# Toeplitz loads issued by ScalarE instead of SyncE, and the wait for a last store moved into the next phase

## The chip, the cores and the metric

The kernel runs on one core of a Trainium2 chip. Its time is the device time of one execution in microseconds, the median of several runs. All five engines are used: TensorE (PE) for matrix products and transposes, VectorE (DVE), ScalarE (ACT), GpSimd (POOL), and SyncE (SP), which only issues transfers. ScalarE and GpSimd issue transfers too, each over its own queue.

## The reference, cut to what matters

`x` is 8 x 256 x 512. Four residual blocks follow one another:

```
x = x + tanh(g_xattn[0]) * conv_mix(ctx, ctx, layernorm(x), ssm_kernel, D)      # long convolution, 32 heads of 8 channels (8 x 32 = 256), over the last axis
x = x + tanh(g_ffn[0])   * moe(layernorm(x))        # 8 experts, top 2, and a shared expert
x = x + tanh(g_xattn[1]) * linear_attention(layernorm(x), ctx)
x = x + tanh(g_ffn[1])   * soft_moe(layernorm(x))

conv_mix: kv[i,j] = k[i] * v[j] per head;  y = causal convolution of kv[i,j] with the head's kernel, over the last axis
          out = sum over i of (y[i,j] + kv[i,j] * D) * q[i]
moe:      w = two largest softmax router scores, normed to 1
          out = sum over the two experts of w_e * (silu(x @ gate_e) * (x @ up_e)) @ down_e  +  shared expert(x)
```

The change touches the first block and the seam between the shared expert and the routed experts of the second. What is computed stays the same.

## The kernel before, in words

The phases run one after another, each in a block of its own: every engine has its own program in it, and the next phase begins when all five have come to the end of theirs.

**Convolution stage** (`conv_stage`, from L142). The convolution is a matrix product with a Toeplitz matrix, built by a transfer that reads the reversed kernel of a head once per partition, each time one element further on (`toeplitz`, L229). One such transfer brings the rows of one step: two heads, high and low fp16 halves, 512 KB into one of the two buffers of `toep`. There are 16 steps. Per step:

- VectorE makes the products of channel pairs (`pairs`, L400 and L402), two steps ahead.
- ScalarE rounds them to fp16 (`split`, L346, `prod_hi`), GpSimd makes the remainder (L304, `prod_lo`).
- TensorE convolves in four blocks m = 0 to 3, of 6, 12, 18 and 24 products (`convolve`, L511 to L513). Block 0 alone waits for the step's Toeplitz rows (L503) and for `prod_lo` (L504). After each block comes an `add_up` (L524) of the block two before. Results go through a ring of three PSUM buffers. In steps 1 to 4 there are also transposes of the later inputs (L496).
- VectorE weighs each block with the query (`weigh`, L428 to L431) and after the third block of a step adds the rows of the step before to the residual (`add_rows`, L440, semaphore `added`).
- Beside this, 24 pieces of the routed experts' down weights are split: GpSimd loads them (L287), ScalarE rounds (`split_parts`, L354), GpSimd makes the remainder (L293) and stores (L295).

The order in each queue is written out by hand. SyncE's is L268 to L273. In step s it issues the Toeplitz load of step s + 2, once step s has been convolved (`conv_done`); then, once `added` says so, the eight stores of step s (L255) and the eight residual loads of step s + 2 (L246). ScalarE's is L364 to L373: root or transposed inputs in a few steps, `split(s + 2)`, `split_parts(s)`. The first two Toeplitz loads it issues itself, at the start (L330).

**Shared phase** (`shared_phase`, from L553). Four chunks of 512 tokens go through the shared expert. In the last one VectorE also works out the routing: `choose`, `lay_out`, `slots` (each slot's number, and `behind`, a comparison of 128x1280 elements, L869), then, after the chunk's last `h` (L913), `places`, and `tokens` (L881), which feed the list of tokens (L1008) that the experts gather by. ScalarE rounds `h` to `h_hi` (L747), GpSimd makes `h_lo` (L782), and TensorE's last products (L1001 to L1003) need it. `add_out` (L897, L899) ends a token tile, and SyncE stores a chunk of four (L702). `x1_in` holds the chunks with odd number, the last among them. At the end SyncE waits for all these stores (L703) and those of the normed rows (L704).

**Expert phase** (`expert_phase`, from L1012). 39 tiles of 128 gathered rows (L1085) are transposed by a transfer (L1263) and go through their expert. What the shared phase stored last is read only by the phase after it.

Of the kernel before, what the change touches and what calls it, by code (L numbers as in the profile page):

```python
# [15 lines left out]
ALU = mybir.AluOpType  # L16
AX = mybir.AxisListType

P = 128
B, N, D = 8, 256, 512  # L20
T = B * N
TT = T // P
KD = D // P
CH = 4 * P
NCH = T // CH
# [93 lines left out]
STEPS = SSM_H // 2  # L119
# [22 lines left out]
def conv_stage(nc, k, x, ctx, ssm_reversed, ssm_d, g_xattn, g_ffn, ssm_split, x1, down, down_whole, down_tail):  # L142
# [5 lines left out]
    with phase(nc) as st:  # L148
# [80 lines left out]
        def toeplitz(eng, s):  # L229


            src = bass.AP(tensor=ssm_split.tensor, offset=s * (4 * PAD), ap=[[1, P], [PAD, 4], [1, D]])
            eng.dma_start(toep[:, s % T_BUFS].rearrange("p e q d -> p (e q) d"), src).then_inc(toep_loaded[s % T_BUFS], 16)

        @block.sync
        def _(sp):
            def load(t, g, u):
                for e in range(2):
                    src = (c_t if t == "c" else x_t)[g, e, :, u * 4:u * 4 + 4, :]
                    sp.dma_start(rows[t][e * 64:e * 64 + 64, u * 4:u * 4 + 4, :], src).then_inc(loaded[t][u], 16)  # L240

            def load_res(s):
                if s >= 2:
                    sp.wait_ge(added, s - 1)
                for j in range(SSM_I):
                    sp.dma_start(res[j * 16:j * 16 + 16, s % 2, :], x_s[s, j]).then_inc(res_loaded[s % 2], 16)  # L246

            def load_toeplitz(s):
                sp.wait_ge(conv_done, (s - T_BUFS + 1) * KD)
                toeplitz(sp, s)  # L250

            def store(s):
                sp.wait_ge(added, s + 1)
                for j in range(SSM_I):
                    sp.dma_start(x1_s[s, j], gated[j * 16:j * 16 + 16, s % 2, :]).then_inc(stored[s % 2], 16)  # L255

            for t in "cq":
                for u in range(2):
                    load(t, 0, u)
            load_res(0)  # L260
            load_res(1)
            for u in range(2):
                sp.wait_ge(turned["c"], 2 * u + 2)
                load("c", 1, u)
            for u in range(2):
                sp.wait_ge(normed, 4 * u + 4)
                load("q", 1, u)
            for s in range(STEPS):  # L268
                if s + T_BUFS < STEPS:
                    load_toeplitz(s + T_BUFS)  # L270
                store(s)
                if s + 2 < STEPS:
                    load_res(s + 2)  # L273
            for u in range(2):
                sp.wait_ge(stored[u], STEPS // 2 * 128)
# [40 lines left out]
        @block.scalar  # L316
        def _(act):
            act.dma_start(ssm[:, :], ssm_reversed).then_inc(ssm_loaded, 16)
            act.dma_start(d_col[:, :], ssm_d.rearrange("(h o) -> h o", o=1)).then_inc(ssm_loaded, 16)
            act.dma_start(k.gates[:, 0:2], g_xattn.partition_broadcast(P)).then_inc(gates_loaded, 16)  # L320
            act.dma_start(k.gates[:, 2:4], g_ffn.partition_broadcast(P)).then_inc(gates_loaded, 16)
            act.wait_ge(gates_loaded, 32)
            nc.scalar.activation(k.tanh_gates[:, :], k.gates[:, :], ACT.Tanh).then_inc(gates_ready, 1)
            act.wait_ge(d_added, 1)
            nc.scalar.activation(ssm_q[:, 0, :], ssm[:, :], ACT.Copy).then_inc(ssm_hi, 1)
            nc.scalar.preload_act_table(ACT.Sqrt)
            act.wait_ge(ssm_lo, 1)
            act.dma_start(ssm_split.rearrange("s e q d -> e s (q d)"), ssm_q[:, :, :].rearrange("h q d -> h (q d)")).then_inc(ssm_stored, 16)
            act.wait_ge(ssm_stored, 16)
            for s in range(T_BUFS):  # L330
                toeplitz(act, s)

            def put(unit):

                act.wait_ge(turned[unit[0]], unit[1] * 4 + unit[2] + 1)
                for half in range(1 if unit in by_dve else 2):
                    for dst, src in turned_in(unit, half):
                        last = nc.scalar.activation(dst, src, ACT.Copy)
                last.then_inc(out_act, 1)

            def split(s):
                u = s % 2
                act.wait_ge(prod_done, s + 1)
                if s >= 2:
                    act.wait_ge(conv_done, (s - 1) * KD)
                nc.scalar.activation(prod_hi[:, u].rearrange("p k e r -> p (k e r)"), prod[:, u, :], ACT.Copy).then_inc(hi_done, 1)  # L346

            def split_parts(s):
                for n in parts_of(s):
                    v, rows_, _, _ = part(n)  # L350
                    act.wait_ge(part_loaded[v], (n // PART_BUFS + 1) * 16)
                    if n >= PART_BUFS:
                        act.wait_ge(part_stored[v], n // PART_BUFS * 16)
                    nc.scalar.activation(part_q[0:rows_, v, 0, :], part_in[0:rows_, v, :], ACT.Copy).then_inc(part_hi, 1)  # L354

            for n in range(4):
                put(("c", 0, n))
            split(0)
            for n in range(2):
                ln.root(nc, act, n)  # L360
                put(("q", 0, 2 * n))
                put(("q", 0, 2 * n + 1))
            split(1)
            for s in range(STEPS):  # L364
                if s in (2, 3):
                    ln.root(nc, act, s)
                if s in later:
                    t, first = later[s]
                    put((t, 1, first))
                    put((t, 1, first + 1))  # L370
                if s + 2 < STEPS:
                    split(s + 2)
                split_parts(s)  # L373
# [179 lines left out]
def shared_phase(nc, k, w, x1, xn_out, x1s, router_t, gate, up, down_whole, down_tail, s_gate, s_gate_b, s_up, s_up_b, s_down, s_down_b):  # L553


    C = 2 * TT
    LAST = NCH - 1
    ETAIL = I_MOE - 2 * P
    with phase(nc) as st:
# [13 lines left out]
        xn = lent(2 * 4 * D).bitcast(F32).rearrange("p (t d) -> p t d", t=4)  # L573
        xq = lent(4 * 2 * D).rearrange("p (t q d) -> p t q d", t=4, q=2)
        assert taken[0] == home.shape[1]
        x_in = [x_first, sb("x1_in", [P, 4, D])[:, :, :]]
        su_hi, su_lo = sb("su_hi", [P, KD, I_SH], F16), sb("su_lo", [P, KD, I_SH], F16)
        sd_hi, sd_lo = sb("sd_hi", [P, SK, D], F16), sb("sd_lo", [P, SK, D], F16)
        rw, rw_hi, rw_lo = sb("rw", [P, KD, E]), sb("rw_hi", [P, KD, E], F16), sb("rw_lo", [P, KD, E], F16)
# [39 lines left out]
        routed, logits_read = sem("routed"), sem("logits_read")  # L619
        gu_done, silu_done, h_done = sem("gu_done"), sem("silu_done"), sem("h_done")  # L620
        h_hi_done, h_lo_done = sem("h_hi_done"), sem("h_lo_done")
        down_done, bias_added, out_done, out_stored = sem("down_done"), sem("bias_added"), sem("out_done"), sem("out_stored")
        consts_made, before_zeroed, chain = sem("consts_made"), sem("before_zeroed"), sem("route_chain")
        e2_done, picked_done, ranked = sem("e2_done"), sem("picked_done"), sem("ranked")
        gap_done, tokens_at, listed = sem("gap_done"), sem("tokens_at"), sem("listed")
# [34 lines left out]
        def _(sp):  # L660
# [26 lines left out]
            for c in range(NCH):  # L687
# [12 lines left out]
                        load_piece(c + 1, i)  # L700
                sp.wait_ge(out_done, (c + 1) * 4)
                sp.dma_start(x1s_d[:, c * 4:c * 4 + 4, :], x_in[u]).then_inc(out_stored, 16)  # L702
            sp.wait_ge(out_stored, NCH * 16)  # L703
            sp.wait_ge(xn_stored, NCH * 16)  # L704

        @block.scalar
# [82 lines left out]
        def _(dve):  # L789
# [3 lines left out]
            def then(*made):  # L793

                for m in made:
                    m.then_inc(chain, 1)
                done[0] += len(made)
                dve.wait_ge(chain, done[0])
# [64 lines left out]
            def slots():  # L863

                then(*(V.tensor_tensor(placed[n][:, :, :], place[:, :, :], pick[n][:, :, :], ALU.mult) for n in range(2)))
                then(*(V.tensor_reduce(slot_f[:, n, :], placed[n][:, :, :], AX.X, ALU.add) for n in range(2)))
                slot = slot_f[:, :, :].rearrange("p n t -> p (n t)")
                then(V.tensor_copy(k.slots[:, :, :], slot_f[:, :, :]),
                     V.tensor_tensor(behind[:, :, :], slot.unsqueeze(2).to_broadcast([P, C, TILES + 1]),  # L869
                                     edges[:, :].unsqueeze(1).to_broadcast([P, C, TILES + 1]), ALU.is_ge))  # L870

            def places():

                slot = slot_f[:, :, :].rearrange("p n t -> p (n t)")
                then(V.tensor_reduce(behind_count[:, :], behind[:, :, :], AX.X, ALU.add),
                     V.tensor_tensor(in_tile[:, :, 0:TILES], behind[:, :, 0:TILES], behind[:, :, 1:TILES + 1], ALU.subtract))
                then(V.scalar_tensor_tensor(in_place[:, :], behind_count[:, :], -float(P), slot, ALU.mult, ALU.add))
# [134 lines left out]
def expert_phase(nc, k, w, xn, y_out, mu, mu_split):  # L1012
# [7 lines left out]
    with phase(nc) as st:  # L1020
# [212 lines left out]
        def _(sp):  # L1233
# [35 lines left out]
            for n in range(TILES, FIRST + PERIOD * (NJ - 1) + 13 + KD):  # L1269
                background(n)  # L1270
            sp.wait_ge(MU["stored"], NJ * KD * 16)
            for u in range(U):
                sp.wait_ge(stored[u], TILES // U * 16)

# [1065 lines left out]
def transformer(nc, a, out):  # L2340
# [11 lines left out]
    with ExitStack() as whole:  # L2352
# [9 lines left out]
        with ExitStack() as routed:  # L2362
            sb, _, _ = opener(nc, routed)
            k.slots, k.mix = sb("slots", [P, 2, TT], I32), sb("mix", [P, 2, TT])
            with ExitStack() as st:
# [4 lines left out]
                w.gate_hi, w.gate_lo, w.up_hi, w.up_lo = (sb(f"w_{n}", [P, E, KD, I_MOE], F16) for n in ("gate_hi", "gate_lo", "up_hi", "up_lo"))  # L2370
                w.down = sb("w_down", [P, 2, E, MK, D], F16)
                w.down_hi, w.down_lo = w.down[:, 0], w.down[:, 1]
                w.down_loaded = nc.alloc_semaphore("w_down_loaded")
                shared_phase(nc, k, w, x1, xn, x1s, a["router_t"], a[F + "gate_w"], a[F + "up_w"], down_whole, down_tail, a[F + "s_gate_w"],
                             a["s_gate_b_cols"], a[F + "s_up_w"], a["s_up_b_cols"], a[F + "s_down_w"], a[F + "s_down_b"])
                expert_phase(nc, k, w, xn, expert_rows, a["L1_ffn_mu"], mu_split)
# [47 lines left out]
```

## Time and profile before

| | us |
|---|---|
| median of 3 runs | 1850.38 |
| lowest, highest | 1847.68, 1852.98 |
| profiled execution | 1857.93 |
| its span, first to last instruction | 1856.2 |
| convolution stage, its steps 5 to 15 | 134 to 291 |
| last store of the shared phase issued | 541.39 |
| first instruction of the expert phase | 546.76 |

| engine | busy us | share |
|---|---|---|
| PE | 1593.5 | 86% |
| DVE | 1107.5 | 60% |
| ACT | 736.5 | 40% |
| POOL | 510.2 | 27% |

The span is the time from the first instruction to the last in one execution that the hardware profiler recorded. Busy time is what an engine spent in instructions; issuing a transfer does not count. Matmuls overlap in their pipeline, so the start of one against the start of the next is the better measure. "PE clock" is the granted clock as a share of 2.4 GHz.

### The profile page before, as it was taken

What the parts mean: (1) busy time and instruction counts of PE and PEld (TensorE: products, weight loads), DVE (VectorE), ACT (ScalarE), POOL (GpSimd) and SP (SyncE); (2) the same over time, 40 slices, a digit from 0 to 9 for tenths busy, and PEclk for the clock granted to TensorE, in tenths of its full rate; (3) what the DMA queues carried; (4) which work ended last, traced back from release to release, by engine and by line L of the source; (5) the groups of instructions that cost most, each with busy time, mean ns of one, the idle gap of its engine ahead of it and who ended that gap; (6) DMA issues with size and microseconds to landing.
All of it is one profiled execution on the core that took longest, in us unless ns stands there. A gap on an engine that the chain in (4) does not pass through costs nothing. (4 is left out here: it accounts for less than half of the span.)

```text
span 1856.2 us, 27893 instructions
## 1 busy us (share of the span) xinstructions
PE 1593.5 (86%) x9596; PEld 931.4 (50%) x9596; DVE 1107.5 (60%) x2218; ACT 736.5 (40%) x1390; POOL 510.2 (27%) x428
## 2 busy tenths in 40 slices
PE   2878884899969999948888886579999999999997
PEld 1767673344426666624444443245555555555554
DVE  4977864534562322246857666566757667676663
ACT  2331211433311332224433332274656656565562
POOL 2446560433322444224424233102011020101000
PEclk7899987999989999969989998789999999999998
DMA  9323433433457576454344222850514325041341
GB/s 194 107 81 123 137 132 117 148 120 110 139 172 184 140 172 172 108 215 154 91 131 118 87 88 83 335 110 12 118 38 87 74 50 125 17 108 43 71 78 48
DMA packets 274301, 215.21 MB, mean 116 GB/s; under 512 B 184770, under 2 KB 223170, under 8 KB 272530
## 3 DMA queue, kind: packets, MB, share of 16 engines
q1 hardware_dynamic: 240288, 159.87, 32.2%
q0 software_dynamic: 9264, 30.15, 5.5%
q10 hardware_dynamic: 24642, 23.76, 4.3%
q8 instruction: 66, 1.08, 0.2%
q14 instruction: 41, 0.34, 0.1%
HBM read 120.33 MB, written 49.63 MB: 92 GB/s over the span
## 5 line engine op out<-in xcount | busy, mean ns | idle before, releaser
L2019 POOL TENSOR_TENSOR s_h_lo<-s_h,s_h_hi 128x512 f16<-128x512 f32 x32 | 37.0, 1155 | 553.0 <-DVE s_h_hi L2230 553.0
L511 PE MATMUL ring<-prod_hi,toep 128*128 128x288 f16 x320 | 95.7, 299 | 34.9 <-DVE terms L431 19.5
L1207 DVE TENSOR_TENSOR e_h<-e_up,e_silu 128x352 f32<-128x352 f32 x39 | 20.5, 525 | 153.8 <-ACT e_silu L1166 143.1
L304 POOL TENSOR_TENSOR prod_lo<-prod,prod_hi 128x2304 f16<-128x2304 f32 x16 | 73.2, 4575 | 134.4 <-ACT prod_hi L346 134.4
L2248 PE MATMUL s_ring<-w_mu,s_xt_hi 128*128 128x512 f16 x256 | 99.0, 387 | 3.6 <-DVE s_xt_lo L2151 3.1
L2250 PE MATMUL s_ring<-w_mu,s_xt_lo 128*128 128x512 f16 x256 | 98.5, 385 | 0.0
L2249 PE MATMUL s_ring<-w_mu,s_xt_hi 128*128 128x512 f16 x256 | 98.4, 385 | 0.0
L2248 PE MATMUL s_acc<-w_w,s_g_hi 128*128 128x512 f16 x256 | 97.1, 379 | 0.2
L2248 PE MATMUL s_ring<-w_w,s_xt_hi 128*128 128x512 f16 x256 | 97.0, 379 | 0.0
L2249 PE MATMUL s_ring<-w_w,s_xt_hi 128*128 128x512 f16 x256 | 97.0, 379 | 0.0
L2250 PE MATMUL s_ring<-w_w,s_xt_lo 128*128 128x512 f16 x256 | 97.0, 379 | 0.0
L2250 PE MATMUL s_acc<-w_w,s_g_lo 128*128 128x512 f16 x256 | 97.0, 379 | 0.0
L2249 PE MATMUL s_acc<-w_w,s_g_hi 128*128 128x512 f16 x256 | 97.0, 379 | 0.0
L2156 DVE TENSOR_REDUCE s_top<-s_lg 128x1 f32<-128x512 f32 x64 | 43.9, 686 | 88.7 <-ACT s_lg L2062 88.5
L512 PE MATMUL ring<-prod_lo,toep 128*128 128x288 f16 x320 | 95.6, 299 | 0.0
L513 PE MATMUL ring<-prod_hi,toep 128*128 128x288 f16 x320 | 95.5, 298 | 0.0
L428 DVE TENSOR_TENSOR terms<-ring,q_e 128x512 f32<-128x512 f32 x64 | 66.9, 1045 | 45.3 <-PE ring L513 43.2
L1166 ACT ACTIVATE e_silu<-e_gate 128x352 f32<-128x352 f32 x39 | 18.1, 464 | 174.9 <-PE e_up L1109 166.3
L2068 ACT ACTIVATE s_dt<-s_ring,s_slot_low 128x256 f32<-128x256 f32 x128 | 59.5, 470 | 53.0 <-DVE s_dq L2178 52.7
L346 ACT ACTIVATE prod_hi<-prod 128x2304 f16<-128x2304 f32 x16 | 34.1, 2132 | 114.6 <-DVE prod L402 114.6
L2233 DVE TENSOR_TENSOR s_g_lo<-s_ring,s_g_hi 128x512 f16<-128x512 f32 x64 | 43.6, 690 | 58.8 <-ACT s_g_hi L2099 58.7
L524 PE MATMUL rows_total<-ident,terms 128*128 128x128 f32 x576 | 78.0, 284 | 0.4 <-DVE terms L431 0.3
(377 smaller groups left out, 4763.7 us busy)
## 6 DMA issues: line engine op xcount, KB each, us to landing
expert_rows<-e_y SPq DMA_DIRECT2D x39, 256.0 KB
a_part_in<-in_L_ffn_W ACTq DMA_DIRECT2D x32, 256.0 KB
w_split<-a_part_q ACTq DMA_DIRECT2D x32, 256.0 KB, 2.5
w_w<-w_split SPq DMA_DIRECT2D x8, 1024.0 KB, 15.0
toep<-ssm_split SPq DMA_DIRECT2D x14, 512.0 KB, 7.4
stage<-in_L_ffn_gate_w SPq DMA_DIRECT2D x8, 704.0 KB
stage<-in_L_ffn_up_w SPq DMA_DIRECT2D x8, 704.0 KB
c_rows<-in_ctx SPq DMA_DIRECT2D x8, 512.0 KB, 11.3
```

The lines of the kernel that those rows point to most:

```text
L304: nc.gpsimd.tensor_tensor(prod_lo[:, u].rearrange("p k e r -> p (k e r)"), prod[:, u, :], prod_hi[:, u].rearrange("p k e r -> p (k e r)"), ...
L428: nc.vector.tensor_tensor(to(0, (9, 4), (1, 8)), values(0, (8, 4), (1, 8)), weights(0, (0, 4), (1, 8)), ALU.mult)
L511: nc.tensor.matmul(out, w_hi, hi, start=(n == 0), stop=False)
L512: nc.tensor.matmul(out, w_hi, lo, start=False, stop=False)
L513: last = nc.tensor.matmul(out, w_lo, hi, start=False, stop=(n == m))
L524: last = nc.tensor.matmul(out, terms[:, n % M_BUFS, o * 8:o * 8 + 8].rearrange("p j n -> p (j n)"), k.ident[:, :], is_transpose=True, star ...
L2068: last_ = A(dt[:, n % 2, e, :], ring[:, bank, e * N:(e + 1) * N], ACT.Exp, bias=slot_low[:, n % 4, e:e + 1], accum_out=slot_sum[:, 2 * n + ...
L2156: V.tensor_reduce(top[:, t, j:j + 1], lg[:, t, j * D:(j + 1) * D], AX.X, ALU.max).then_inc(S["top_done"], 1)
L2233: V.tensor_tensor(g[1][:, n % G_BUFS, :], ring[:, bank, :], g[0][:, n % G_BUFS, :], ALU.subtract).then_inc(S["g_lo"], 1)
L2248: mm(out_, a[0], b_[0], start=first, stop=False)
L2249: mm(out_, a[0], b_[1], start=False, stop=False)
L2250: return mm(out_, a[1], b_[0], start=False, stop=last_)
```

## The change

Three things. The Toeplitz loads of steps 2 to 15 leave SyncE's queue; ScalarE issues each of them at the top of the step before the one that needs it. The wait for the stores of `x1s` leaves the end of the shared phase and stands at the end of the expert phase; for this the buffer `x1_in` and the semaphore live on over both. And `behind` is computed in `places`, after the last `h`, instead of in `slots`, ahead of it.

```diff
@@ conv_stage, sync
-            def load_toeplitz(s):
-                sp.wait_ge(conv_done, (s - T_BUFS + 1) * KD)
-                toeplitz(sp, s)
...
             for s in range(STEPS):
-                if s + T_BUFS < STEPS:
-                    load_toeplitz(s + T_BUFS)
                 store(s)
                 if s + 2 < STEPS:
                     load_res(s + 2)
@@ conv_stage, scalar
             for s in range(STEPS):
+                if s >= 1 and s - 1 + T_BUFS < STEPS:
+                    act.wait_ge(conv_done, s * KD)
+                    toeplitz(act, s - 1 + T_BUFS)
                 if s in (2, 3):
                     ln.root(nc, act, s)
@@ shared_phase
-        x_in = [x_first, sb("x1_in", [P, 4, D])[:, :, :]]
+        x_in = [x_first, w.x1_in[:, :, :]]
...
-        down_done, bias_added, out_done, out_stored = sem("down_done"), sem("bias_added"), sem("out_done"), sem("out_stored")
+        down_done, bias_added, out_done, out_stored = sem("down_done"), sem("bias_added"), sem("out_done"), w.x1s_stored
@@ shared_phase, sync
-            sp.wait_ge(out_stored, NCH * 16)
             sp.wait_ge(xn_stored, NCH * 16)
@@ shared_phase, vector: slots() and places()
-                slot = slot_f[:, :, :].rearrange("p n t -> p (n t)")
-                then(V.tensor_copy(k.slots[:, :, :], slot_f[:, :, :]),
-                     V.tensor_tensor(behind[:, :, :], slot.unsqueeze(2).to_broadcast([P, C, TILES + 1]),
-                                     edges[:, :].unsqueeze(1).to_broadcast([P, C, TILES + 1]), ALU.is_ge))
+                then(V.tensor_copy(k.slots[:, :, :], slot_f[:, :, :]))
 
             def places():
 
                 slot = slot_f[:, :, :].rearrange("p n t -> p (n t)")
+                then(V.tensor_tensor(behind[:, :, :], slot.unsqueeze(2).to_broadcast([P, C, TILES + 1]),
+                                     edges[:, :].unsqueeze(1).to_broadcast([P, C, TILES + 1]), ALU.is_ge))
@@ expert_phase, sync
             sp.wait_ge(MU["stored"], NJ * KD * 16)
+            sp.wait_ge(w.x1s_stored, NCH * 16)
@@ transformer
-                w.down_loaded = nc.alloc_semaphore("w_down_loaded")
+                w.x1_in = sb("x1_in", [P, 4, D])
+                w.down_loaded, w.x1s_stored = nc.alloc_semaphore("w_down_loaded"), nc.alloc_semaphore("x1s_stored")
```

## Rows read from the trace of the kernel before

**Rows 1.** Busy time by stretch: length, engines, granted clock, share of DMA, GB/s.

```profile
20.00:34.00 14.00, 1.97 (x8) 1.57 (x8) 5.77 (x8) 5.36 (x9) 0.00 (x0) 0.50 0.87 192
...
134.00:148.90 14.90, 11.44 (x96) 9.84 (x97) 10.79 (x19) 5.42 (x6) 7.66 (x5) 1.00 0.35 111
...
232.90:247.20 14.30, 14.11 (x96) 11.56 (x97) 8.89 (x16) 0.00 (x0) 7.59 (x7) 0.81 0.43 137
...
134.00:291.00 157.00, 135.70 (x1074) 115.36 (x1074) 115.29 (x206) 30.72 (x29) 86.78 (x61) 0.95 0.38 123
```

**Rows 2.** Timeline of TensorE at boundaries of steps: start, length, instruction, idle before.

```profile
130.32 1.15 PE L524 MATMUL rows_total<-ident,terms 128*128 128x128 f32 x9
131.30 1.04 PE L496 MATMUL ring<-ident,xq 128*128 128x128 f32 x8
134.33 0.28 PE L511 MATMUL ring<-prod_hi,toep 128*128 128x288 f16 x1 [1.99 <-DVE terms L431]
...
204.97 0.28 PE L511 MATMUL ring<-prod_hi,toep 128*128 128x288 f16 x1 [1.34 <-issue]
...
215.27 1.15 PE L524 MATMUL rows_total<-ident,terms 128*128 128x128 f32 x9
217.33 0.28 PE L511 MATMUL ring<-prod_hi,toep 128*128 128x288 f16 x1 [0.91 <-issue]
...
232.93 0.40 PE L511 MATMUL ring<-prod_hi,toep 128*128 128x288 f16 x1 [4.16 <-issue]
...
276.53 0.28 PE L511 MATMUL ring<-prod_hi,toep 128*128 128x288 f16 x1 [1.30 <-DVE terms L431]
```

**Rows 3.** Timeline of SyncE's queue, step 10.

```profile
206.25 5.20 SPq L246 DMA_DIRECT2D res<-in_x  x8
211.50 0.41 SPq L233 DMA_DIRECT2D toep<-ssm_split  x1
```

**Rows 4.** Toeplitz loads, us to landing: step 11's; SyncE's in 130:291; ScalarE's first pair.

```profile
toep<-ssm_split SPq DMA_DIRECT2D x1, 512.0 KB, 5.7
...
DMA to landing us min/median/max: 5.7/8.8/10.1
...
DMA to landing us min/median/max: 13.2/16.2/19.1
```

**Rows 5.** Timeline of ScalarE in step 9.

```profile
203.85 2.12 ACT L346 ACTIVATE prod_hi<-prod 128x2304 f16<-128x2304 f32 x1 [12.79 <-DVE prod L402]
205.88 1.14 ACT L354 ACTIVATE part_q<-part_in 128x512 f16<-128x512 f32 x2
```

**Rows 6.** Timeline of VectorE: the products in two steps.

```profile
184.68 3.38 DVE L400 TENSOR_TENSOR prod<-c_e 128x2048 f32<-128x2048 f32 x1
...
201.21 2.27 DVE L400 TENSOR_TENSOR prod<-c_e 128x2048 f32<-128x2048 f32 x1
```

**Rows 7.** Timeline of GpSimd's transfers.

```profile
212.08 0.68 POOL L295 DMA_DIRECT2D down_whole<-part_q  x1 [0.30 <-POOL part_q L293]
```

**Rows 8.** End of the shared phase: last store, its time to landing, next phase's first instruction.

```profile
541.39 0.37 SPq L702 DMA_DIRECT2D after_shared<-x_in  x1
...
after_shared<-x_in SPq DMA_DIRECT2D x1, 1024.0 KB, 4.3
...
546.76 0.10 POOL L1080 MEMSET e_ones<- 128x1 f32 x1 [21.09 <-POOLq L36]
```

**Rows 9.** Timeline of VectorE, then GpSimd, around the last `h`.

```profile
520.27 1.48 DVE L869 TENSOR_TENSOR behind<-slot_f,edges 128x1280 f16<-128x1280 f32 x1
521.79 0.74 DVE L913 SCALAR_TENSOR_TENSOR silu_h<-gu,bu,silu_h 64x512 f32<-64x512 f32 x1
...
524.71 1.02 DVE L877 SCALAR_TENSOR_TENSOR in_place<-behind_count,slot_f 128x32 f32<-128x32 f32 x1
525.78 4.19 DVE L881 TENSOR_SCALAR silu_h<-row,in_place,token 128x128 f16<-128x128 f32 x16
...
523.27 2.41 POOL L782 TENSOR_TENSOR h_lo<-silu_h,h_hi 64x512 f16<-64x512 f32 x1 [3.99 <-ACT h_hi L747]
```

## The prediction

> **What bounds the kernel now.** I first looked for the two places that the change touches, then at who waits there. The first is the convolution stage, 16 steps. I call (s,m) the matmuls of step s and block m; each step is (s,0) to (s,3), with one `add_up` (L524) after each block.
>
> The table by stretch [rows 1] says that over steps 5 to 15 (134 to 291 us) TensorE is busy 135.7 us of 157, VectorE 115.3, ScalarE 30.7, and the DMA engines 38%. TensorE leads but is not full, so the question is what stops it. Its timeline at the step boundaries [rows 2] answers: step 10 begins at 204.97 and its last `add_up` at 215.27. Elsewhere what follows an `add_up` starts 0.98 us after that one's start (130.32 to 131.30). A step that waits for nothing thus takes 215.27 + 0.98 - 204.97 = 11.28 us. But (11,0) starts at 217.33, 1.08 late, and (12,0) at 232.93, with 4.16 us of idleness that the profile calls "issue": no engine released it. What (s,0) needs and no other block does is the Toeplitz load `toep` of step s and `prod_lo`. `prod_lo` of step 11 started on GpSimd at about 206 and runs 4.6, so it was long there. SyncE issued `toep` of step 11 at 211.50 [rows 3] and it landed 5.7 us later [rows 4], at 217.2; the matmul came at 217.33. All eleven loads of steps 5 to 15 stand like this, the matmul 0.1 us behind the landing. So the load ends every step's wait.
>
> Why it is issued so late is in [rows 3]: SyncE first issues the eight stores of the step before, then the eight residual loads (5.20 us, to 211.45), then `toep` at 211.50. Its own condition, that step 9 had released the buffer, had held since about 203.
>
> The sum of what this costs: (5,0) starts at 134.33 and (15,0) at 276.53 [rows 2], 142.2 us for ten steps, against 10 x 11.28 = 112.8. 29.4 us are lost. Before (5,0) eight transposes stand at 131.30 (1.04 long), after which the matmuls could have started at about 132.25; they start at 134.33, which is 2.1 more. Together 31.5 us. Part of that is clock: a stretch behind the longest wait shows the granted clock at 0.81 instead of 1.00 [rows 1], so the engine ran part of them at 1.2 GHz instead of 2.4. It is so in the steps that follow waits of 3.3 us or more (6, 9, 12 and 14). From the start of (s,0) to the end of (s,3) the other steps take 10.46 us, these four 7.6 us more in all; the waits themselves are the remaining 23.9.
>
> **The change, part by part.**
>
> *Toeplitz loads to ScalarE.* At the top of step s ScalarE waits for `conv_done` at 4s and issues the load of step s+1. The wait costs nothing: the copy `prod_hi` just ahead of it on the same queue already waits for the same count. What stands ahead of the load is that copy and the one or two `part_q` copies. For step 11 that is 203.85 to 205.97 and then 205.88 + 1.14 = 207.02 [rows 5]. So the load goes out at 207.05 instead of 211.50, 4.45 us earlier. Step 11 could use it at 216.25. Of those 9.2 us, 1.5 come from the wait ahead of (10,0), which would be gone; that leaves a window of 7.7 us (0.5 more in steps with one part). A load that takes L makes the next step wait L - 7.7, less what the step before it waited.
>
> L is the unknown. On SyncE's queue it is 5.7 at least, 8.8 in the middle and 10.1 at most in this stretch [rows 4]. With 5.7 nothing is left. With 8.8 the waits would alternate between 1.1 and 0, 6 us in 11 steps. With 10.1 they would be 13 us. Waits that short have no slow stretch behind them in this trace. For the lower end speaks that GpSimd's part transfers (256 KB out at 212.08, then 256 KB in) [rows 7] start within 0.6 us of the old issue, and 5 us after the new one; against it that SyncE's eight residual loads (206.25 to 211.45) now run beside it. I take 3 us in all, nearer to the shortest load. Gain here: 31.5 - 3 = 28.5, bounds 18.5 and 31.5.
>
> The Trainium skill ("DMA: Bandwidth & Descriptors", section "Issuing engines are not separate DMA queues") speaks against hoping for more: all queues share the same 16 DMA engines, and another issuer saves only issue time, "usually small relative to the DMA itself". By it L would stay at 8.8 and this part give 25.5; the 4.45 us of earlier issue are what counts, and those the trace shows directly.
>
> What else the move costs: 0.4 to 0.8 us of issue on ScalarE, 14 times, beside idle stretches of 9 to 15 us ahead of each `prod_hi`; nothing. If that cover were gone it would be 6 us. On SyncE 0.41 us go, after which it waits for `added` anyway. In steps 1 to 4 the load of step 2 comes later than before (64.6 instead of 59.4, needed at 73.7), the others 2 to 3 us earlier; they were not waited for. An L above 9 would cost up to 1 us once.
>
> What is late next? VectorE. From start to start it needs 4 x 1.79 for the weighing, 0.65 for the gated rows and 2.53 for the products, 10.3 us; where GpSimd works beside it the product takes 3.38 instead of 2.27 [rows 6], 11.4. With that in every other step the mean is 10.9, under TensorE's 11.28. At worst every step is 11.4: 2 us in all. `prod_lo` of a step ends about 4 us ahead of its use.
>
> *Last store outside the phase.* SyncE issues the last store at 541.39 (0.37 us), it lands 4.3 us later, at 545.7, and the next phase's first instruction is at 546.76 [rows 8], 1.07 after. Without the wait the phase begins at 541.39 + 0.37 + 1.07 = 542.8: 3.9 us. The expert phase starts with a chain (gather, transposing load, first matmul at 555.80) that then moves whole. The store's bytes move in about 542 to 545; the first gather's, 1.7 us or so after an issue at 543.6, hardly meet them. Bounds: 2.5 if they meet or code comes late, 3.9 if not. I take 3.9.
>
> *`behind` moved.* It ran 520.27 to 521.75, ahead of the last `h` (521.79) [rows 9]. Now `h` goes first, when its `silu` is there (520.8), 0.9 us earlier. `h_hi` and `h_lo` follow, for which TensorE stood idle 2.3 us. VectorE's own work does not shrink: `behind` stands between `h` and the reductions, 0.4 us later for the hole ahead of `h`, and `in_place` takes 1.02 us only because it overlaps GpSimd's `h_lo` (523.27, 2.41 long instead of 1.16). If `h_lo` gets through early, the tokens start at 525.5 instead of 525.78, and as the list is ready sooner another 0.56 us go: 0.7 gained. If VectorE and GpSimd take turns, 1.48 + 1.47 + 0.83 + 0.2 + 1.16 after 521.55 is 526.7: 0.9 lost. I take 0.
>
> The Trainium skill ("SBUF — State Buffer", section "SBUF: two separate sides") has a rule for the second case: a VectorE operation with two SBUF inputs and a GpSimd operation exclude one another for their whole length. `behind` has two SBUF inputs. By it this edit would cost 0.9. The 2.41 and 1.02 us in the trace agree with it.
>
> **Sum.** 28.5 + 3.9 + 0 = 32.4 us. Against the profiled execution: 1857.9 - 32.4 = 1825.5. That execution lies 7.5 us over the median of the plain runs, 1850.4; I take the same difference there: 1818.0. If part of the 7.5 us is longer landings under the profiler, the plain runs have less to win, up to that much. The later phases only shift.
>
> **Rivals.**
>
> 1. *The load lands no faster and meets the residual loads* (L of 10 to 12). Waits of 13 to 23 us stay, without much slow clock: gain 8.5 to 18.5, plus 3.9. About 1833 with L near 11. For it: 10.1 has been seen, and the stores and loads of SyncE are in flight at the new time. Against: these move only 32 KB each 0.65 us. 0.13.
>
> 2. *Slower: ScalarE's queue is served last.* The only two loads that went over it before landed in 13.2 and 19.1 us [rows 4], beside heavy traffic of SyncE's queue. With 16.2 the waits would be 8.5 us every other step, 47 us in all, with some 9 us of slow clock behind them: 56 against 31.5. Then 1850.4 + 24.5 - 3.9 = 1871. It decides from L = 13.4 on, where waits and slow clock equal today's. Against: the DMA engines were then 87% busy, here 38% [rows 1]. 0.05.
>
> 3. *The plain runs have no such waits*, or another release takes their place at once (VectorE, or a slow clock for another reason); only the phase's end is won: 1846.5. Against: the landing and the matmul stand together eleven times. 0.05.
>
> 4. *The waits go mostly, but the edits around the phase's end lose*: VectorE and GpSimd take turns (0.9), code of the next phase comes late (1.4), and 3 us more of waits stay: 1823. 0.12.
>
> **How the numbers follow.** The forecast, 1818, has 0.65, its own span 1813 to 1825. The lower end of the range is all waits gone and 0.7 from `behind`: 1814, and 2 for the difference between profile and plain runs: 1812. The upper end takes in rival 4 and most of rival 1: 1835. A measurement of this kernel can tell about 0.3%, 5.5 us. Faster by more: forecast, 1 and 4, 0.90; within: rival 3, 0.05; slower: rival 2, 0.05.
>
> **What would show it.** Right: in the changed profile the boundaries (s,3) to (s,0) lie 11.3 us apart for steps 5 to 15, granted clock 1.00 there, (15,0) near 248; `toep` issued by ScalarE right behind `part_q` and landed in under 8 us; the first gather about 2.2 us behind the last store's issue instead of 6.15. Wrong: "issue" idleness left ahead of L511, landings above 10 us on ScalarE's queue, or VectorE without gaps in the stage and TensorE waiting for `terms`.

## The result: 1840.7 us, a third of the gain that was forecast

The changed kernel takes 1840.72 us, the median of 7 runs (1837.18 to 1843.36), against 1850.38 us for the kernel before, again 7 runs (1846.65 to 1853.02). The ratio is 0.9943, with an interval of 0.993 to 0.9955: 9.7 us faster, where 32.4 were forecast. The direction was right, the size was not; the measured time lies above the range of 1812 to 1835.

The profiled execution of the changed kernel took 1837.18 us, with a span of 1835.5. From here "before" and "after" are the two kernels; line numbers of after are a few lower. One of the runs named below, one of e2, took 1853.22 us at a granted clock of 0.902, where the others have 0.94 to 0.96, and is left out of the median there.

**What went as predicted.** First the loads themselves. These are a row of after's page (issues, count, size, us to landing), then three of ScalarE's timeline in step 10 (start, length, instruction):

```profile
toep<-ssm_split ACTq DMA_DIRECT2D x16, 512.0 KB, 8.0
```

```profile
190.52 2.12 ACT L340 ACTIVATE prod_hi<-prod 128x2304 f16<-128x2304 f32 x1 [11.41 <-DVE prod L399]
190.70 0.37 ACTq L233 DMA_DIRECT2D toep<-ssm_split  x1
192.55 1.14 ACT L348 ACTIVATE part_q<-part_in 128x512 f16<-128x512 f32 x2
```

The load even goes out 0.18 us after `prod_hi` has started, not behind `part_q` as I had put it: both `part_q` copies stand ahead of it in the program, and they begin only at 192.55. Here ScalarE's queue issues a DMA whose own wait is met while the instructions ahead of it have yet to compute. The load lands about 8 us later. The waits ahead of the first matmul of a step are gone. Steps 5 to 7 run at the pace of the forecast: (5,0) starts at 128.62, (6,0) at 140.05, (7,0) at 151.33, (8,0) at 162.74, or 11.4 us a step.

Then the end of the shared phase, on SyncE's queue and on GpSimd, which answers to [rows 8]:

```profile
532.06 0.37 SPq L699 DMA_DIRECT2D after_shared<-x_in  x1
```

```profile
533.57 0.10 POOL L1075 MEMSET e_ones<- 128x1 f32 x1 [18.07 <-POOLq L36]
```

From the store's issue to the next phase's first instruction there are 1.51 us instead of 5.37: 3.86 us gained, 3.9 forecast.

**What didn't.** Step 8 still takes 11.28 us, step 9 takes 12.43, and steps 10 to 14 take 14.06, 13.22, 14.09, 13.18 and 14.02. (15,0) starts at 255.02, so the seven steps from 8 on take 92.28 us, 13.2 in the mean; at 11.28 each it would have been 79. The table by stretch answers to [rows 1] (columns: length; busy time and instructions of TensorE's matmuls, TensorE's weight loads, VectorE, ScalarE and GpSimd; granted clock; DMA share; GB/s):

```profile
134.00:281.00 147.00, 122.64 (x1031) 105.23 (x1029) 109.80 (x199) 28.20 (x26) 86.37 (x61) 0.97 0.37 126
162.70:255.00 92.30, 80.29 (x674) 68.62 (x673) 71.51 (x133) 21.12 (x19) 56.26 (x38) 1.00 0.40 134
```

Between 162.7 and 255 TensorE stands idle for 12.0 us of 92.3 at a granted clock of 1.00, its upper level of 2.4 GHz, so this is waiting and not clock. The waits of 134:281 say for what (columns: total us, times, longest):

```profile
PEld rows_total L521 <- DVE terms L428: 18.1, 8, 4.1
PE rows_total L521 <- DVE terms L428: 15.9, 7, 3.9
DVE gated L437 <- issue: 14.7, 5, 5.2
...
DVE gated L437 <- PE rows_total L521: 10.6, 3, 3.5
DVE gated L437 <- DMA res<-in_x: 8.3, 1, 8.3
```

TensorE waits for VectorE (`terms`), and VectorE waits ahead of `gated`: 33.6 us in nine pieces, for steps 7 to 15. Before had 1.3 us of that. Behind `gated` on VectorE's queue stand the products and the weighing that TensorE needs. VectorE's timeline around 200 us shows one such place:

```profile
197.50 0.26 DVE L428 TENSOR_TENSOR terms<-ring,q_e 128x64 f32<-128x64 f32 x1
200.42 0.75 DVE L437 SCALAR_TENSOR_TENSOR gated<-rows_total,tanh_gates,res 128x512 f32<-128x512 f32 x1 [2.67 <-issue]
201.09 2.28 DVE L397 TENSOR_TENSOR prod<-c_e 128x2048 f32<-128x2048 f32 x1
203.29 0.42 DVE L399 TENSOR_TENSOR prod<-c_e 128x256 f32<-128x256 f32 x1
203.62 1.03 DVE L425 TENSOR_TENSOR terms<-ring,q_e 128x512 f32<-128x512 f32 x1
```

`gated` reads `rows_total` and the residual rows `res`. The label names TensorE for three of these waits and nothing ("issue") for five. The semaphore records of the trace tell more: the last piece of `res` for this one landed at 200.34, and `gated` started at 200.42. It is so for all nine: `gated` starts 0.08 us behind the landing of its step's last residual rows. Those of step 9, which this `gated` reads, were issued by SyncE from 183.16 to 189.98, as its timeline shows, which answers to [rows 3]:

```profile
161.12 7.57 SPq L251 DMA_DIRECT2D after_conv<-gated  x8
168.73 6.71 SPq L246 DMA_DIRECT2D res<-in_x  x8
175.48 7.63 SPq L251 DMA_DIRECT2D after_conv<-gated  x8
183.16 6.82 SPq L246 DMA_DIRECT2D res<-in_x  x8
190.02 6.28 SPq L251 DMA_DIRECT2D after_conv<-gated  x8
196.35 7.09 SPq L246 DMA_DIRECT2D res<-in_x  x8
```

Two things are to be seen. Eight issues take 6.2 to 7.6 us here; before they took 4.89 (stores) and 5.20 (loads, [rows 3]). And the row that ends one eight is followed at once by the next: from 149 us on, until the loads end at 271, SyncE's queue is never idle.

How late the rows land shows a backlog that grows. I take the time from the end of the eighth residual issue of a step to the landing of its last row. For steps 5, 6 and 7 it is 6.9, 9.3 and 11.7 us, from then on 10.3 to 11.7, and 8.6 for the last. Step 5's `gated` still had 5.8 us to spare, step 6's 2.5, step 7's nothing. So steps 5 to 8 of TensorE keep the forecast pace while the backlog fills, and the later ones don't.

**And the end of the stage.** Seven of the nine waits, 20.0 us, lie between 162.7 and 255 and leave TensorE idle for the 12.0 us. The last two, 5.19 and 8.33 us, stand at the end, for steps 14 and 15, when TensorE has little or nothing left to do. The last:

```profile
279.58 0.75 DVE L437 SCALAR_TENSOR_TENSOR gated<-rows_total,tanh_gates,res 128x512 f32<-128x512 f32 x1 [8.33 <-DMA res<-in_x]
```

| us | (5,0) | (15,0) | first transfer of the next phase |
|---|---|---|---|
| before | 134.33 | 276.53 | 300.00 |
| after | 128.62 | 255.02 | 290.90 |
| e1 (below) | 132.75 | 246.20 | 268.04 |
| e4 (below), stage as in before | 130.04 | 268.54 | 294.02 |

At (15,0) after is 21.5 us ahead of before, at the end of the stage 9.1; ahead of e4 it is 13.5 and 3.1. More than half of what the steps won is lost there, by the same backlog.

Why the rows land so late stands in the DMA view of one step of after, 202 to 215 us (40 equal slices: tenths of all 16 DMA engines busy, and GB/s):

```profile
DMA  3197257513999934111131111111111111596194
GB/s 139 50 328 277 88 151 296 227 57 123 293 378 378 337 98 161 47 50 50 47 104 50 50 50 41 50 47 47 47 50 44 50 50 50 227 397 227 50 227 189
```

There are bursts (the Toeplitz load and GpSimd's parts, up to 397 GB/s) and between them a floor: one tenth of the engines busy, mostly 47 to 50 GB/s. Before has the same floor. This is 3 us of before in which only SyncE's residual loads and stores were under way:

```profile
DMA  1111110111110111111101111101111111011111
GB/s 55 55 55 55 55 55 27 55 55 55 55 55 27 55 55 55 55 55 55 55 27 55 55 55 55 55 27 55 55 55 55 55 55 55 27 55 55 55 55 55
...
q1 hardware_dynamic: 85, 0.15, 13.3%
```

13.3% of 16 engines is 2.1 engines: these transfers run on two of the sixteen. The packet records agree: from 134 to 255 us before and after mostly have two rows of 2 KB in flight at a time, and never more than four. Each transfer moves 16 rows of 2 KB, and its side in DRAM is cut as [2][8] rows.

The Trainium skill has the rule for it ("DMA: Bandwidth & Descriptors", section "Why a DMA increments its semaphore by 16 and not by 1"): a transfer uses as many engines as the largest number up to 16 that divides the slowest dimension of both of its sides, and when SyncE or ScalarE issues it, these are the lowest-numbered ones. For [2][8] that is 2. The trace agrees, with its 13.3%. The page is cited here for how many; what that costs is measured next.

### The profile page after: what moved, and what is told of

It reads as the page before. It is cut to its first block and busy times, and to the rows that moved or that the text cites. A ratio compares the mean times of both kernels' runs of the same rounds, so it can differ in the third digit from the quotient of the medians.

```text
span 1835.5 us, 27892 instructions
## 1 busy us (share of the span) xinstructions
PE 1575.6 (86%) x9596; PEld 921.9 (50%) x9596; DVE 1101.7 (60%) x2218; ACT 737.2 (40%) x1390; POOL 512.7 (28%) x428
## 5 line engine op out<-in xcount | busy, mean ns | idle before, releaser
L508 PE MATMUL ring<-prod_hi,toep 128*128 128x288 f16 x320 | 92.6, 289 | 12.6 <-DVE terms L428 12.6
L510 PE MATMUL ring<-prod_hi,toep 128*128 128x288 f16 x320 | 92.5, 289 | 0.0
L521 PEld LDWEIGHTS rows_total<-ident,terms 128*128 128x128 f32 x576 | 66.1, 142 | 20.0 <-DVE terms L428 18.6
## 6 DMA issues: line engine op xcount, KB each, us to landing
c_rows<-in_ctx SPq DMA_DIRECT2D x8, 512.0 KB, 10.2
```

Source lines behind the costliest of these rows:

```text
L508: nc.tensor.matmul(out, w_hi, hi, start=(n == 0), stop=False)
L510: last = nc.tensor.matmul(out, w_lo, hi, start=False, stop=(n == m))
L521: last = nc.tensor.matmul(out, terms[:, n % M_BUFS, o * 8:o * 8 + 8].rearrange("p j n -> p (j n)"), k.ident[:, :], is_transpose=True, star ...
```

## The experiments

**Theory A (two DMA engines).** The two engines have more work in a step than TensorE. A step stores and loads 256 rows of 2 KB over two engines. At the floor of 50 GB/s, 25 rows a us, this is 10.2 us. A sixteenth of the Toeplitz load lies on each engine, so two carry 64 KB of it, 1.3 us at the same rate, and 1.3 us for each part that goes in and out (256 KB each way), one or two a step. Together 12.8 us in a step with one part and 14.1 in one with two, an estimate from those rates. Once the backlog stands, the steps of after alternate in this way: 13.2 us where ScalarE rounds one part (11 and 13), 14.1 where it rounds two (10 and 12). **Theory B** was that the second queue itself slows SyncE's issue. **Theory C** was that what counts is the sum of issue and transfer costs, so that relieving half of the transfers gives half.

**e1: after, with the rows cut otherwise.** Each transfer still has 16 rows of 2 KB, as many of them as before, but the loop index now names a batch, and the DRAM side becomes [8][2].

```diff
+        x_b, x1_b = (a.rearrange("b (e s j) d -> s b j e d", e=2, j=SSM_I) for a in (x, x1))
-                    sp.dma_start(res[j * 16:j * 16 + 16, s % 2, :], x_s[s, j])
+                    sp.dma_start(res[j:P:B, s % 2, :], x_b[s, j])
-                    sp.dma_start(x1_s[s, j], gated[j * 16:j * 16 + 16, s % 2, :])
+                    sp.dma_start(x1_b[s, j], gated[j:P:B, s % 2, :])
```

> The changed kernel with the residual loads and the stores of the convolution stage cut another way: each of the eight takes one batch b and all 16 pairs (j, e), instead of one j and all 16 pairs (e, b). Same count, bytes and rows of 2 KB. Theory A (two DMA engines are the bound): as they were cut, such a transfer runs on only 2 of the 16 DMA engines, 25 rows a microsecond; 256 rows a step are 10.2 us, and with these two engines' share of the Toeplitz load and the parts 14 us, which is the step of both kernels. Cut the new way it runs on 8. Then steps 5 to 15 take TensorE's 11.3 us instead of about 14 (the last seven), VectorE no longer waits ahead of the gated rows, SyncE's eight issues take 4.9 to 5.2 us again instead of 6 to 7.6, and the time is some 20 us below the changed kernel's, near 1821. Theory B (the order of issue, or the second queue's descriptors, slow SyncE): the bytes per DMA engine don't matter, steps stay near 14 us and the time stays within 3 us of 1841.

Measured: 1814.8 us (5 runs, 1811.31 to 1819.72), ratio to before 0.9802 [0.9782, 0.9822]. Beside the 9.7 us of the change this is 26 us more. From (5,0) to (15,0) it is 132.75 to 246.20, 11.35 us a step; the prediction gave TensorE 11.28. The stage by stretch, and the waits of VectorE ahead of `gated` in it:

```profile
134.00:260.00 126.00, 125.81 (x1065) 108.84 (x1063) 115.57 (x209) 31.31 (x30) 91.71 (x61) 1.00 0.50 152
```

```profile
DVE gated L438 <- PE rows_total L522: 1.3, 1, 1.3
```

TensorE is busy 125.81 of 126.00 us. SyncE's eights, with ScalarE's queue as active as in after:

```profile
169.72 5.06 SPq L247 DMA_DIRECT2D res<-in_x  x8
176.04 4.95 SPq L252 DMA_DIRECT2D after_conv<-gated  x8
181.03 5.06 SPq L247 DMA_DIRECT2D res<-in_x  x8
187.43 4.91 SPq L252 DMA_DIRECT2D after_conv<-gated  x8
```

They are back at 4.9 and 5.1 us, with holes of 1.3 us between. So theory B falls: with the second queue as active as in after, SyncE's eights are short again. What held them was the backlog on the two engines. The rows of a step now land 1.4 to 2.2 us behind the last issue instead of 10.3 to 11.7, and up to eight rows, for moments ten, are in flight at a time. The recut also changes which partitions a transfer touches. That this helped would show in the rows, and a row of 2 KB takes the same time in both, a median of 0.084 us. And the DMA view of one step (200.8 to 213.8) has no floor any more, and slices with nothing in them:

```profile
DMA  7852331288899999995573430321000025982597
GB/s 252 328 202 63 132 114 32 76 66 126 214 350 280 230 277 397 416 404 208 196 233 107 95 82 13 88 57 38 6 0 0 0 50 202 429 246 76 145 290 303
```

```profile
toep<-ssm_split ACTq DMA_DIRECT2D x16, 512.0 KB, 5.8
```

The Toeplitz load lands in 5.8 us instead of 8.0: the share of it that lies on the two engines had queued behind SyncE's rows. e2 shows the same for the 5.7 to 10.1 us that it took before, [rows 4].

**e2: before, with the same cut.** The old order of issue, the new cut.

> The kernel before with the same recut of residual loads and stores alone. Theory A: the Toeplitz load on SyncE's queue loses its tail (its last 64 rows of 1 KB, which sat on the two loaded engines) and lands in about 4.5 to 5.5 us instead of 8.8; waits of about 1 us a step are left because it is still issued late, steps of about 12.2 us instead of 14.2, time 1850 - 20 = 1830. Theory B: the order of issue is what counts, the steps stay at 14.2 us, 1850.

Measured: 1827.9 us (median of 4, 1820.69 to 1828.84), 0.9862 [0.9839, 0.9885]. (15,0) stands at 249.72, (5,0) at 129.79: 12.0 us a step. The landing, on its page:

```profile
toep<-ssm_split SPq DMA_DIRECT2D x14, 512.0 KB, 3.9
```

Of the lateness in before, then, the larger part was not when the load was issued but how long it took behind the other rows on two engines. With 3.9 us to landing (3.5 to 5.1 in the stage), SyncE's late issue leaves only 0.7 us a step.

**e3: the Toeplitz part of the change alone.** The end of the shared phase is as in before. The diff is cut to SyncE's side; ScalarE's three lines are those of the change.

```diff
-            def load_toeplitz(s):
-                sp.wait_ge(conv_done, (s - T_BUFS + 1) * KD)
-                toeplitz(sp, s)
...
-                if s + T_BUFS < STEPS:
-                    load_toeplitz(s + T_BUFS)
```

> The kernel before with the Toeplitz loads on ScalarE's queue and nothing else of the change. Both theories: this part alone gave the changed kernel's 9 us in its convolution stage and nothing after, so 1841 + 4 = about 1845.

Measured: 1843.6 us (6 runs), 0.996 [0.9945, 0.9975], 7.0 us less than before, which had a median of 1850.59 (17 runs) beside e1 to e4. The step pattern is after's: (8,0) at 165.97, (15,0) at 259.98, 13.4 each, with these waits of VectorE in 134:281:

```profile
DVE gated L437 <- PE rows_total L521: 14.3, 4, 3.7
DVE terms L425 <- PE ring L510: 9.1, 9, 1.6
DVE gated L437 <- issue: 4.6, 4, 1.7
```

**e4: the end of the phase alone.** After, with the Toeplitz loads back on SyncE as in before.

> The changed kernel with the Toeplitz loads back on SyncE's queue: the wait for the last store in the expert phase and the comparison after the last h are left. The gap from the last store's issue to the expert phase's first instruction is 1.5 us instead of 5.4, and the end of the shared phase 0.3 us shorter; 1850 - 4.2 = about 1846. If the two parts don't add up (this and the Toeplitz move alone together give more or less than the whole change's 9.7 us), the rest comes from somewhere else.

Measured: 1846.79 us (12 runs), 0.998 [0.9968, 0.9993]: 3.8 us less. Parts and whole agree within what these medians can tell: 7.0 + 3.8 = 10.8 against 9.7.

**e5 and e6: only half of the rows recut.** e5 recuts the residual loads alone, e6 the stores alone, both on top of after. They separate theory A from C: if the two engines bound a step only while they have more work than TensorE, either half brings the step under TensorE's 11.3 us (128 rows are 5.1 us at the floor's rate, plus the 2.6 to 3.9 of the others), and the gain is whole both times.

> The changed kernel with only the residual loads cut the new way; the stores keep the old cut. Theory A (two DMA engines are the bound): 128 of the 256 rows a step leave those two engines, 5.1 us less apart from their new share of 0.6 to 1.3; about 10 of the 14 us stay, which is under TensorE's 11.3. So a threshold, not a sum: nearly the whole gain of the full recut, steps of 11.3 to 11.8 us, time 1815 to 1820. Theory C (each kind of transfer costs by its own, by where its rows lie in memory): half of the full recut's 26 us, 1828.

> The changed kernel with only the stores cut the new way. Theory A: the same threshold, steps of 11.3 to 11.8 us; and at the stage's end the last 16 stores go out at 0.6 us each instead of 0.9, 4 us more than the loads alone give; 1815 to 1819. Theory C: the other half, 1828.

Measured: e5 1814.86 us (4 runs), 0.9803 [0.9772, 0.9834]; e6 1813.19 us (4 runs), 0.9797 [0.9775, 0.9819]. Each has the whole gain of e1, and theory C falls. SyncE's queue in e5, in the stretch where after had eights of 7 us:

```profile
172.46 4.96 SPq L252 DMA_DIRECT2D after_conv<-gated  x8
177.45 5.08 SPq L247 DMA_DIRECT2D res<-in_x  x8
183.86 5.22 SPq L252 DMA_DIRECT2D after_conv<-gated  x8
```

(15,0) stands at 242.62 in e5, from 129.14 at (5,0), and at 243.29 from 129.81 in e6: 11.35 us a step in both. The Toeplitz load lands in 8.2 us in e5 and 5.1 in e6, and it makes no difference, since ScalarE's early issue leaves a window of over 8 us. The expectation for e6 had the last 16 stores of after at 0.9 us each. They are not: the row of 16 in after, 14.23 us from 270.96, is two eights of 4.91 and 4.83 us with 4.49 us between them, in which SyncE waits for step 15's `gated`. e1, e5 and e6 can't be told from one another; any of them beats both kernels, by 26 to 28 us against after.

**e7 and e8: the two edits at the end of the phase, one by one.** e7 is before with `behind` moved behind the last `h`; e8 is before with the last store's wait moved into the next phase and `behind` left where it was. One run each, so only the distances inside the profile are read.

> The kernel before with only the comparison moved behind the last h. From the start of the product of places and picks to the issue of the last store it was 23.2 us before and 22.9 in the changed kernel. If the two engines take turns it would be 24.1; if h_lo gets through early, 22.5. I expect 22.9, and 5.4 us from the last store to the next phase, as before.

> The kernel before with only the wait for the last store moved into the expert phase: 1.5 us instead of 5.4 from the last store's issue to the expert phase's first instruction, the first expert matmul about 4 us earlier behind it, 23.2 us ahead of it as before.

Measured: e7 1853.22 us, e8 1847.13 us. From the start of `tie` to the last store's issue it is 23.2 us in before, 22.47 in e7, 23.2 in e8, 22.55 in e4 and 22.89 in after. From the store to the next phase's first instruction it is 5.37 in before, 5.39 in e7, and 1.51 in e8, e4 and after. So the wait is the whole of the 3.9 us, and `behind` gives 0.3 to 0.7. Its rows in e7 answer to [rows 9]:

```profile
522.38 0.74 DVE L912 SCALAR_TENSOR_TENSOR silu_h<-gu,bu,silu_h 64x512 f32<-64x512 f32 x1 [0.58 <-ACT silu_h L739]
523.04 1.47 DVE L872 TENSOR_TENSOR behind<-slot_f,edges 128x1280 f16<-128x1280 f32 x1
524.55 1.49 DVE L874 TENSOR_REDUCE behind_count<-behind 128x32 f32<-128x1280 f16 x1
...
526.82 0.19 DVE L876 SCALAR_TENSOR_TENSOR in_place<-behind_count,slot_f 128x32 f32<-128x32 f32 x1
...
523.86 1.67 POOL L782 TENSOR_TENSOR h_lo<-silu_h,h_hi 64x512 f16<-64x512 f32 x1 [3.14 <-ACT h_hi L747]
```

## Why the prediction was wrong, step by step

1. *"Why it is issued so late", and "So the load ends every step's wait".* The readings held: the wait for `toep` was there, and the change took it away. What I did not ask is whether the late issue was the only thing at its limit. Under it lay a second one, two DMA engines with 13 to 14 us of rows a step. The step in before, 14.2 us (13.85 in e4, which has the same stage), lay less than one us above that limit, the 13.7 us that steps 10 to 14 of after take in the mean. Moving the issue could win TensorE much time only while the backlog filled, and the end of the stage gave most of that back. The table by stretch had hidden it: 38% of the DMA engines busy is an average over sixteen, and two of them can be full in it.

2. *"L is the unknown."* This was the right unknown and the wrong reason. I explained the spread of 5.7 to 10.1 us by GpSimd's parts. e1 and e2 show what it was: with SyncE's rows on eight engines the same load lands in 5.8 us from ScalarE's queue and 3.9 from SyncE's. On ScalarE's queue in after it is 8.0, and 8.0 was covered, since the load also went out about 3 us earlier than I had it, behind the start of `prod_hi` and not behind `part_q`. This step cost nothing in the end, which is partly luck.

3. *"On SyncE 0.41 us go, after which it waits for `added` anyway", and "these move only 32 KB each 0.65 us".* This is the step that failed, and rival 1 was set aside by the second of these sentences. I took 5.2 us for eight residual loads as what SyncE needs whatever happens, and their transfer as hidden. But 256 such rows a step are 10.2 us on two engines. As soon as SyncE no longer stood waiting for `added`, the backlog there grew, and the eights went from 4.9 and 5.2 us to between 6.2 and 7.6. The `res` rows of a step, landed 9.7 to 13.5 us ahead of `gated` in before, then came later than TensorE's sums, and `gated` waited 33.6 us.

4. *"What is late next? VectorE."* TensorE does wait for VectorE in after, but not because VectorE is full, as I had it (2 us at worst): it is busy 71.51 us of 92.3. It stands waiting for a transfer, with the work that TensorE needs behind this wait on its queue. "VectorE without gaps" as the sign of a miss was the wrong sign; the sign was gaps ahead of `gated`.

5. *The conv term of the sum, 28.5 us (bounds 18.5 to 31.5).* It measured 7.0 (e3). With the second limit gone, e1 gives 35.8 us in all, and less 3.9 at the phase's end that is 31.9, about the whole of the 31.5 us that I had counted as lost (the cut itself is part of it; e2 alone gives 22.7). The count of what a free step takes, 11.28 us, was right to 0.07 us. Rival 1 had the right kind of waits, at the wrong place and for the wrong transfer; its 1833 was nearer than the forecast and still too low.

6. *The last store.* 3.9 forecast, 3.86 in the profile, 3.8 by e4, which has the 0.3 to 0.7 of `behind` in it. Right, with its mechanism: the first instruction and the first gather (534.34) follow the store's issue by 1.51 and 2.28 us, as forecast.

7. *`behind`.* I took 0, between a gain of 0.7 and a loss of 0.9; 0.3 in after and 0.7 in e7, the end of the range where `h_lo` gets through early. The loss of 0.9 did not come, though the rows fit engines that take turns. In e7 `h_lo` starts at 523.86 with 0.65 us of `behind` left and takes 1.67 us, of which 1.02 lie behind `behind`'s end; a wait for the rest and then the 1.16 that it takes alone would be 1.81. What I had wrong is who pays: I let VectorE stand still for these 1.16 us, but they passed beside the reduction, which took 1.49 us as against 1.47 before, and `in_place` took 0.19 us instead of 1.02.

8. *The link from the profile to the median.* Before's profiled execution lay 7.5 us over its median, after's 3.5 us below. The two profiles differ by 20.7 us of span, of which the convolution stage has 9.1 and the phase's end about 4; some 5 lie in the attention phase, which the change doesn't touch (359.9 us from 803.0 to 1162.9 before, 354.7 from 789.2 to 1143.9 after). e4, with the old order of issue, ends its convolution stage 6 us earlier than before's profile. One profile's stage is thus good to some 6 us; the gains above are from medians for that reason, and the distances at the end of the stage are given against both before and e4.

What stays open: how large a backlog a queue takes before it holds up its issues (eight still took 5.2 us with rows landing 9.3 us behind them, the loads for step 6 of after), and whether four engines would do as well as eight. No run varied either.

## What to carry to other kernels

When a transfer is found late, look at how many DMA engines it and its neighbours run on before you look at when it is issued: a stretch in which the DMA share stands at one tenth and the rate at 50 GB/s, slice after slice, was two full engines here, while the mean share said 38%. Before's own trace had a second sign: the residual rows landed 4.1 to 8.7 us behind the last of their eight issues, where e2, with the other cut, has 1.5 to 1.6. And when a wait is taken away, price each resource by the work it has in a step and not by the time that its rows now show; a queue that used to wait showed here the pace of issue without a long backlog. A recut of the transfers, with the same number of instructions and bytes, was worth 22.7 us by itself and 26 on top of the change, where the change gave 9.7.

## What was not expected of the hardware

- A row of 2 KB takes 0.08 us on a DMA engine whichever way the rows are cut (median packet time 0.084 us before, after and in e1). Two engines reach 25 to 26 rows in a us; in e1 up to 75 were seen in one. The rows had not become cheaper, only more of them went at a time.
- Where the rows landed 10 us and more behind their issue, the issues took longer too: 6.2 to 7.6 us for eight instead of 4.9 to 5.2, and unevenly. Between 258 and 265 us of after most stores took 0.57 us each, and one took 2.17:

```profile
258.58 2.17 SPq L251 DMA_DIRECT2D after_conv<-gated  x1
```

- ScalarE's queue passes on a DMA 0.1 to 0.2 us after the ACTIVATE ahead of it has begun, 1.9 us before that one ends (190.70 against 190.52 to 192.64). That the DMA's own wait had been met is read from the program: it asks for the same count as the ACTIVATE. An issue at the top of a step is earlier than the timeline of the engine's work suggests.
- The profile's label for a wait on two things can miss a DMA: eight of nine waits ahead of `gated` are put down to "issue" or TensorE, and the landing of the residual rows, 0.08 us ahead of `gated` in all nine, tells what it was.
